# Order around the row maxima of a fused attention and expert kernel: two maxima and their places in the gating, the fourth score unit, and the norm's transposes

## The chip, the cores and the metric

One NeuronCore of a Trainium2 chip runs the whole kernel. The metric is the device time of one execution in microseconds (us). TensorE is called PE here, VectorE DVE, ScalarE ACT, GpSimd POOL, and SyncE, which issues most of the DMAs, SP. L1087 is line 1087 of the kernel before.

## The reference, cut to what matters

The input is x of 32 batch elements x 256 positions x 128 channels, float32. A layer norm gives xn; the output is x + attention(xn) + ffn(xn).

```
def attention(xn):                       # 16 heads of width 8
    q, k, v = split(xn @ Wqkv.T)
    q, k = rotate(q, cos, sin), rotate(k, cos, sin)
    s = q @ k.T / sqrt(8) + decay_bias   # causal
    return softmax(s) @ v @ Wo.T

def ffn(x):
    n1 = layernorm(x)
    rw = gating(n1, smha_sim)            # 8 experts, thresholded cosine, top 2 as fallback, softmax
    q, k, v = (einsum(n1, w, rw) for w in (q_proj, k_proj, v_proj))
    hs = x + einsum(softmax(causal(q @ k.T / sqrt(128))) @ v, o_proj, rw)
    n2 = layernorm(hs)
    rw2 = gating(n2, moe_sim)
    return hs + einsum(gelu(n2 @ w1), w2, rw2)
```

## The kernel before

The kernel is written for each engine as a program of its own, with semaphores between them; the order on each engine is the order of the code. The batch elements pass through a pipeline. `step(n, u, n_x)` is written once for each engine; n is the element, u its parity, and n_x says which later elements still exist (3: all; 29 of the 32 steps). Two steps stand in a hardware loop.

In step n the softmax attention and the expert attention of element n are finished, the row maxima of element n+1 are taken, the gating of element n+2 is worked out, and the norm and the rotated q and k of element n+3 are made.

The 16-head attention takes its scores twice. `unit1` on PE puts scores in PSUM banks S1, and `row_max` on DVE (L1087) reads them; six units of both, numbered 0 to 5, make up an element. A unit needs the S1 banks empty, so PE's unit k+1 waits for DVE's maximum k (`s1_read`), and the maximum k+1 waits for PE (`s1_out`). `max_parts` splits the maxima, and they are fed back as rows of the operands. `unit2` on PE then puts the scores less maxima in banks S2, ACT takes `exp_slot` (L674) and puts the masks back with `seed_slot` (L680); `unit2` k waits for the seed k-1. After three of these `pv` (L1437, L1442) multiplies by v: half 0 and half 1. `ve`, `qk` and `oe` are the weight products of the expert attention, `soft_max` (L1122 to L1125), `soft_exp` (L699, L701) and `soft_T` its softmax.

On DVE the `gating` is a chain of 31 small dependent instructions ("links"; 128x16 elements). `beside_gating(k)` is called behind link k and puts other work between: one instruction of the layer norm's own chain (`layer_norm`, a generator), a row maximum where k stands in `GATE_MAX_AT`, the soft maximum at 15, the normalising of PV's first half at 18. The layer norm's last link, L917, releases POOL's `second_norm` (L572, a product of two SBUF tiles, and the copy L576). `rotate` (L1004 to L1014) turns q and k of element n+3 and splits them into three bf16 parts that SP stores. PE's `norm_T` (L1329) transposes the new norm into bank S1[0], ACT's `evac_norm_x` (L620) copies it to xzT, and `proj` (L1337) and `proj_v` (L1360) multiply it by the weights. At the end of a step DVE's `add_x` waits for `att_out`, and then come `rotate`, the row maximum 0 of the next step's element, and `add_hs` (L1154, L1161).

Of the kernel before, what the change touches and what calls it, by code (L numbers as in the profile page):

```python
# [24 lines left out]
UNITS = 3 * NQ  # L25
# [33 lines left out]
MAX_LINKS = 3  # L59
ATS_CHUNKS = ((0, 1), (1, 1), (2, 2), (4, 2), (6, 2))  # L60
GELU_AT = (2, 7, 12, 17, 22, 27)
GATE_MAX_AT = (2, 7, 11, 14, 17)


class Chain:
# [55 lines left out]
def build(nc, x, w_attn, w_o, log_xi, pi_logit, e_logit, ln1_w, ln1_b, ln2_w, ln2_b, sim1, gates1,  # L121
# [9 lines left out]
    with ExitStack() as ctx:  # L131
# [468 lines left out]
        def _(act):  # L600
# [16 lines left out]

            def evac_norm_x(b, banks):
                act.wait_ge(xzT_out, b + 1)
                act.activation(xzT[:], ps[:, banks[0]].rearrange("p (a t) -> p a t", a=2), ACT.Copy).then_inc(xnT_done, 1)  # L620

            def evac_norm_1(b, par):
# [60 lines left out]
            def exps(n, k):  # L683
                exp_slot(n, k)
                seed_slot(n, k)

            def evac_pv(n, Q):
                act.wait_ge(pv_out, NQ * n + Q + 1)
                act.wait_ge(ot_out, NQ * n + max(Q - 1, 0))
                act.activation(ov[:, Q], ps[:, PVB, 0:S], ACT.Copy).then_inc(ov_done, 1)  # L690

            def evac_qk(n):
                act.wait_ge(qk_out, n + 1)
                act.activation(qT[:], ps[:, QKB, 0:S], ACT.Copy, scale=D ** -0.5).then_inc(qkT_done, 1)
                act.activation(kT[:], ps[:, QKB, S:2 * S], ACT.Copy).then_inc(qkT_done, 1)
# [74 lines left out]
            def step(n, u, n_x):  # L770
                if n_x >= 2:
                    evac_norm_1(n + 2, u)
                exps(n, 0)
                if n_x >= 2:
                    evac_logits(n + 2)
                if n_x == 0:
                    evac_norm2(0)
                    square2(0)
                exps(n, 1)
                if n_x == 0:  # L780
                    evac_norm2(1)
                    square2(1)
                exps(n, 2)
                if n_x == 0:
                    scale_norm2(2)
                    evac_logits2(0)
                evac_qk(n)
                evac_pv(n, 0)
                exps(n, 3)
                if n_x == 0:  # L790
                    scale_norm2(3)
                if n_x >= 2:
                    gate_tanh(n + 2)
                soft_exp(n)
                exps(n, 4)
                if n_x == 0:
                    evac_norm2(2)
                    square2(2)
                    gate_tanh2(0)
                exp_slot(n, 5)  # L800
                evac_soft(n)
                evac_ve(n)
                if n_x:
                    seed_slot(n, 5)
                if n_x == 0:
                    evac_norm2(3)
                    square2(3)
                evac_pv(n, 1)
                if n_x == 3:
                    evac_norm_x(n + 3, LATER)  # L810
                if n_x >= 2:
                    evac_v(n + 2, u)
                if n_x >= 2:
                    evac_weights(n + 2)
                if n_x:
                    evac_max(n + 1)
                evac_att(n)
                if n_x:
                    put_max(n + 1, 1 - u)
                if n_x == 1:  # L820
                    scale_norm2(0)
                    scale_norm2(1)
                if n_x == 0:
                    evac_weights2(0)
                    evac_logits2(1)
# [60 lines left out]
        def _(dve):  # L886
# [113 lines left out]
            def rotate(b, banks):  # L1000
                c = Chain(dve, rot_chain, b, ROT_LINKS)
                both = ps[:, banks[1]].rearrange("p (a t) -> p a t", a=2)
                dve.wait_ge(rot_out, b + 1)
                c.add(dve.tensor_tensor(rott, both, cs[:, :, 0], ALU.mult))  # L1004
                c.add(dve.stream_shuffle(swapped, both, SWAP))
                c.wait()
                c.link(dve.tensor_tensor(swapped, swapped, cs[:, :, 1], ALU.mult))
                c.link(dve.tensor_tensor(rot, rott, swapped, ALU.add))

                dve.wait_ge(parts_stored, 32 * b)  # L1010
                c.link(dve.tensor_copy(parts[:, 0], rot))
                c.link(dve.tensor_tensor(rres, rot, parts[:, 0], ALU.subtract))
                c.link(dve.tensor_copy(parts[:, 1], rres))
                dve.tensor_tensor(parts[:, 2], rres, parts[:, 1], ALU.subtract).then_inc(parts_out, 1)  # L1014
                c.close()
# [62 lines left out]
            def row_max(b, k):  # L1078

                Q, i = divmod(k, 3)  # L1080
                dve.wait_ge(s1_out, UNITS * b + k + 1)
                if k == 0:

                    dve.wait_ge(max_chain, (MAX_LINKS + 1) * b)
                n = HG if i == 0 else 2
                h = HG * Q + (0 if i < 2 else 2)
                dve.tensor_reduce(mx[:, min(i, 1)].rearrange("p (f h) -> p f h", f=NF)[:, :, h:h + n],  # L1087
                                  ps[:, S1[0]:S1[0] + NF].rearrange("p f (h t) -> p f h t", h=n),
                                  AX_X, ALU.max, negate=True).then_inc(s1_read, 1)
# [105 lines left out]
            def step(n, u, n_x):  # L1195
                def next_max(k):
                    if n_x:
                        row_max(n + 1, k)


                norm = (layer_norm(n + 3, 1 - u) if n_x == 3 else layer_norm2(0) if n_x == 1 else
                        layer_norm2(1) if n_x == 0 else iter(()))

                def beside_gating(k):
                    next(norm, None)
                    if k in GATE_MAX_AT:
                        next_max(1 + GATE_MAX_AT.index(k))
                    if k == 15:
                        soft_max(n)
                    if k == 18:  # L1210
                        normalise(n, 0)
                    if k == 28:
                        soft_norm(n)
                if n_x >= 2:
                    for _ in range(3):
                        next(norm, None)
                    gating(n + 2, T, 0, gate1, LG1, NORM1, 1, beside_gating)
                    run(norm)
                else:
                    if n_x == 0:  # L1220
                        run(norm)
                        gating(0, BP, 1, gate2, LG2(0), LG2(0)[:, :, E], 2, beside_gating)
                        run(layer_norm2(2))
                    else:
                        for k in range(1, GATE_LINKS + 1):
                            beside_gating(k)
                        run(norm)
                if n_x:
                    max_parts(n + 1)
                normalise(n, 1)  # L1230
                for e, ne in ATS_CHUNKS:
                    scale_att(n, u, e, ne)
                add_x(n, u)
                if n_x == 3:
                    rotate(n + 3, LATER)
                if n_x >= 2:
                    row_max(n + 2, 0)
                add_hs(n, u)

            for b in range(2):  # L1240
                norm = layer_norm(b + 1, 1 - b)
                rotate(b, FIRST)
                gating(b, T, 0, gate1, LG1, NORM1, 1, lambda k, norm=norm: next(norm, None))
                run(norm)
            for k in range(UNITS):
                row_max(0, k)
            max_parts(0)
            rotate(2, LATER)
            row_max(1, 0)
            step(0, 0, 3)  # L1250
            step(1, 1, 3)
            with dve.Fori(1, NB // 2 - 2) as j:
# [59 lines left out]
        def _(pe):  # L1312
# [173 lines left out]
            def soft_T(n):  # L1486
                pe.wait_ge(sexp_done, 2 * n + 2)
                for k in range(3):
                    ins = pe.transpose(ps[:, G1, k * P:(k + 1) * P], sp[:, k * P:(k + 1) * P], ident[:])
                ins.then_inc(spT_out, 1)  # L1490
# [79 lines left out]
            def step(n, u, n_x):  # L1570
# [28 lines left out]
                qk(n, 6)  # L1599
                next_max(3)  # L1600
                qk(n, 7)
                pv(n, u, 0)
                if n_x == 0:
                    logits2(0)
                next_max(4)
                unit2(n, u, 3)
                soft_scores(n)
                ve(n, 0)
                out_T(n, 0)
# [10 lines left out]
                if n_x == 0:  # L1620
                    norm_T2(3)
                soft_T(n)
                pv(n, u, 1)
                soft_av(n, (lambda: pe.wait_ge(lg_read, f + 1)) if n_x >= 2 else (lambda: None))
                out_T(n, 1)
                if n_x >= 2:
                    proj_v(f, True)
                if n_x == 3:

                    norm_T(g, LATER, lambda: pe.wait_ge(s1_read, UNITS * f))  # L1630
                if n_x >= 2:

                    weights_T(f, lambda: None)
# [147 lines left out]
```

## Time and profile before

| | us |
|---|---|
| median of 3 runs (1326.6 to 1327.27) | 1326.93 |
| the profiled execution | 1325.18 |
| its span, first to last instruction | 1323.4 |
| PE busy (10652 matmuls) | 1172.0, 89% |
| DVE busy | 1029.2, 78% |
| ACT busy | 713.0, 54% |
| POOL busy | 211.5, 16% |

The mean granted clock of TensorE is 0.975 of full speed. The span has three parts: about 90 us of setting up and first elements, the 32 steps to about 1035 us, and then the expert MLP. Busy shares are over the whole span; what sets the time of the steps must be read from one of them.

### The profile page before, as it was taken

The numbers are of one execution on the slowest core, as the hardware profiler recorded it, in microseconds if no ns is written. First come the engines' busy times: TensorE is split into PE (matmuls) and PEld (weight loads), VectorE is DVE, ScalarE is ACT, GpSimd is POOL, SyncE is SP. The second block draws the span as 40 slices with busy tenths as digits, with TensorE's granted clock in tenths as the row PEclk, the third lists the DMA queues.
The fourth block names the chain that finished last, engine by engine and source line by source line (L and its number), as shares of the span: only waits on it lengthen the run. The fifth ranks groups of instructions, "written<-read, shape, count | busy, mean of one in ns | idle before, by whom it ended". The sixth has DMA issues, their size and how long they took to land.

```text
span 1323.4 us, 33513 instructions
## 1 busy us (share of the span) xinstructions
PE 1172.0 (89%) x10652; PEld 900.1 (68%) x10652; DVE 1029.2 (78%) x3723; ACT 713.0 (54%) x1281; POOL 211.5 (16%) x325
## 2 busy tenths in 40 slices
PE   0239999999999999999999999999999979999998
PEld 0117777777777777777777777777777757777776
DVE  6568888888888888888888888888887567777664
ACT  1106655566665556565556665555665855555532
POOL 1021111211122211111221112221111100000000
PEclk9659999999999999999999999999999999999999
DMA  5221333323333332233333233333223034444453
GB/s 136 76 82 43 86 101 103 91 84 86 84 83 86 85 87 81 81 91 99 103 83 87 85 83 84 86 86 85 81 82 114 11 148 161 161 160 161 162 194 141
DMA packets 107941, 133.18 MB, mean 101 GB/s; under 512 B 18116, under 2 KB 87252, under 8 KB 99692
## 3 DMA queue, kind: packets, MB, share of 16 engines
q1 hardware_dynamic: 105668, 131.66, 33.1%
q10 hardware_dynamic: 2216, 0.80, 0.2%
q8 instruction: 31, 0.51, 0.2%
q14 instruction: 26, 0.21, 0.1%
HBM read 109.12 MB, written 21.54 MB: 99 GB/s over the span
## 4 chain that ended last, share of the span: by engine, by line
PE 58%; DVE 18%; ACT 9%; issue 7%; SPq 4%; DMA 2%; DVEq 1%; ACTq 0%
PE ps L1712 9%; PE ps L1698 8%; ACT pr L674 5%; PE ps L1437 5%; PE ps L1460 5%; PE ps L1461 4%; DVE mx L1087 3%; PE ps L1470 3%; PE ps L1506 3%; PE ps L1337 3%; ACT ps L680 3%; PE ps L1442 2%; PE ps L1386 2%; SPq L417 2%; PE ps L1396 2%
## 5 line engine op out<-in xcount | busy, mean ns | idle before, releaser
L674 ACT ACTIVATE pr<-ps 128x1024 f32<-128x1024 f32 x192 | 196.5, 1023 | 159.1 <-PE ps L1420 87.7
L1087 DVE TENSOR_REDUCE mx<-ps 128x4 f32<-128x1024 f32 (+1 forms) x192 | 234.8, 1223 | 56.3 <-PE ps L1396 48.3
L565 POOL TENSOR_TENSOR n1s<-rep,n1T 128x256 f32<-128x256 f32 x256 | 177.4, 729 | 365.7 <-DVE mpart L1101 345.8
L680 ACT ACTIVATE ps<-trn 128x1024 f32<-128x1024 bf16 x191 | 196.6, 1029 | 5.1
L1712 PEld LDWEIGHTS ps<-w2s,ats 128*128 128x128 f32 x1024 | 131.7, 192 | 51.3 <-issue 46.5
L1460 PE MATMUL ps<-n1s,wqk 128*128 128x256 f32 x512 | 163.6, 401 | 0.0
L1461 PE MATMUL ps<-n1s,wqk 128*128 128x256 f32 x512 | 152.9, 380 | 0.0
L858 ACT ACTIVATE n1s<-ps 128x512 f32<-128x512 f32 x128 | 76.5, 597 | 123.2 <-PE ps L1698 122.0
L1470 PE MATMUL ps<-wv,n1s 128*128 128x128 f32 x1024 | 141.6, 281 | 0.0
L1712 PE MATMUL ps<-w2s,ats 128*128 128x128 f32 x1024 | 135.8, 276 | 1.7 <-DVE ats L1269 1.7
L1470 PEld LDWEIGHTS ps<-wv,n1s 128*128 128x128 f32 x1024 | 126.7, 191 | 11.5 <-issue 6.5
L1698 PE MATMUL ps<-rep,w1s 128*128 128x512 f32 x256 | 130.7, 594 | 0.0
L1506 PE MATMUL ps<-wop,ats 128*128 128x128 f32 x1024 | 127.5, 278 | 0.2 <-DVE ats L1138 0.2
L1506 PEld LDWEIGHTS ps<-wop,ats 128*128 128x128 f32 x1024 | 120.9, 193 | 5.6 <-issue 4.9
L1461 PEld LDWEIGHTS ps<-n1s,wqk 128*128 128x128 f32 x512 | 97.8, 191 | 13.5
L1460 PEld LDWEIGHTS ps<-n1s,wqk 128*128 128x128 f32 x512 | 89.0, 194 | 20.8 <-issue 7.6
L572 POOL TENSOR_TENSOR zt<-xn,rstd 128x256 f32<-128x256 f32 x32 | 19.6, 612 | 461.0 <-DVE rstd L917 461.0
L1138 DVE TENSOR_TENSOR ats<-rep,ps 128x512 f32<-128x512 f32 (+1 forms) x160 | 81.1, 573 | 0.0
L1386 PE MATMUL ps<-mask_r,mask_l 64*128 64x256 bf16 x256 | 36.6, 283 | 46.9 <-DVE mx L1087 46.6
L1437 PE MATMUL ps<-pr,vst 128*32 128x256 f32 x1024 | 68.5, 385 | 7.3 <-ACT pr L674 6.6
L1386 PEld LDWEIGHTS ps<-mask_r,mask_l 64*128 64x128 bf16 x256 | 12.3, 93 | 78.7 <-DVE mx L1087 68.0
L620 ACT ACTIVATE xzT<-ps 128x512 f32<-128x512 f32 x32 | 19.1, 597 | 78.4 <-PE ps L1329 78.4
(229 smaller groups left out, 2031.9 us busy)
## 6 DMA issues: line engine op xcount, KB each, us to landing
rep<-scr_rw SPq DMA_DIRECT2D x32, 1024.0 KB, 5.7
stk<-scr_rw SPq DMA_DIRECT2D x16, 1024.0 KB, 8.3
stk<-scr_parts SPq DMA_DIRECT2D x896, 16.0 KB
scr_parts<-parts SPq DMA_DIRECT2D x64, 192.0 KB, 5.9
rots<-scr_rw SPq DMA_DIRECT2D x8, 1024.0 KB, 4.8
wqk<-scr_rw SPq DMA_DIRECT2D x8, 1024.0 KB, 9.1
stk<-scr_parts SPq DMA_DIRECT2D x128, 48.0 KB
xt<-in_x SPq DMA_DIRECT2D x32, 128.0 KB, 2.1
```

The costliest lines, as they stand in the source:

```text
L565: pool.tensor_tensor(n1s[:, e], rep[:, par, e], n1T[:, par], ALU.mult).then_inc(n1s_done, 1)
L674: act.activation(pr[:, Q, :, i], ps[:, S2[0]:S2[0] + NF], ACT.Exp).then_inc(exp_done, 1)
L680: act.activation(ps[:, S2[0]:S2[0] + NF], seeds[:, kind:kind + 1].broadcast_to((P, NF, 512)), ACT.Copy).then_inc(seed_done, 1)
L1087: dve.tensor_reduce(mx[:, min(i, 1)].rearrange("p (f h) -> p f h", f=NF)[:, :, h:h + n], ps[:, S1[0]:S1[0] + NF].rearrange("p f (h t) -> p ...
L1138: dve.tensor_tensor(ats[:, e:e + ne], rep[:, u, e:e + ne], ps[:, G0:G0 + 1, 0:S].broadcast_to((P, ne, S)), ALU.mult).then_inc(ats_done, 1)
L1437: mm(ps[32 * h:32 * h + 32, PVB, 0:S], vst[:, u, 0, HH * f + HG * Q + h], pr[:, Q, f, h // 2, (h % 2) * S:(h % 2 + 1) * S], start=(f == 0) ...
L1460: mm(ps[:, QKB, 0:S], wq[:, e], n1s[:, e], start=(e == 0), stop=(e == E - 1), skip_group_check=True)
L1461: ins = mm(ps[:, QKB, S:2 * S], wk[:, e], n1s[:, e], start=False, stop=(e == E - 1), skip_group_check=True)
L1470: ins = mm(ps[:, QKB, i * D:(i + 1) * D], n1s[:, e, i * P:(i + 1) * P], wv[:, e], start=(e == 0 and i == 0), stop=(e == E - 1), skip_group ...
L1506: ins = mm(ps[:, G1, i * D:(i + 1) * D], ats[:, e, i * P:(i + 1) * P], wop[:, e], start=(e == 0 and i == 0), stop=(e == E - 1), skip_group ...
L1698: mm(ps[:, UP[k % 4]], w1s[:, e], n2T[t % 8], start=True, stop=True).then_inc(up_out, 1)
L1712: ins = mm(ps[:, MOE[t % 2], i * D:(i + 1) * D], hgs[:, k % 2, i * P:(i + 1) * P], w2s[:, e], start=(e == 0 and i == 0), stop=(e == E - 1) ...
```

## The change

The instructions stay the same. What moves:

- DVE: row maximum 0 goes between the rotation and the bf16 parts. `rotate` becomes a generator with one `yield` for this.
- DVE: row maximum 1 goes ahead of the layer norm's statistics and the gating. The maxima 2 to 5 stand behind links 1, 6, 13 and 17; before, 1 to 5 stood behind 2, 7, 11, 14 and 17.
- PE: `unit2` 3 goes ahead of `pv` 0, and `norm_T` ahead of `pv` 1.
- ACT: exponential 3 goes ahead of the copy of `pv` 0, its seed stays behind it. `evac_norm_x` also waits for `proj_v` (`v_out`), which reads the old xzT.

```diff
-GATE_MAX_AT = (2, 7, 11, 14, 17)
+GATE_MAX_AT = (1, 6, 13, 17)
...
             def evac_norm_x(b, banks):
                 act.wait_ge(xzT_out, b + 1)
+
+                act.wait_ge(v_out, b)
...
                 evac_qk(n)
+                exp_slot(n, 3)
                 evac_pv(n, 0)
-                exps(n, 3)
+                seed_slot(n, 3)
...
                 c.link(dve.tensor_tensor(rot, rott, swapped, ALU.add))
+                yield
 
                 dve.wait_ge(parts_stored, 32 * b)
                 c.link(dve.tensor_copy(parts[:, 0], rot))
...
+                next_max(1)
                 norm = (layer_norm(n + 3, 1 - u) if n_x == 3 else layer_norm2(0) if n_x == 1 else
                         layer_norm2(1) if n_x == 0 else iter(()))
 
                 def beside_gating(k):
                     next(norm, None)
                     if k in GATE_MAX_AT:
-                        next_max(1 + GATE_MAX_AT.index(k))
+                        next_max(2 + GATE_MAX_AT.index(k))
...
                 add_x(n, u)
-                if n_x == 3:
-                    rotate(n + 3, LATER)
+                turn = rotate(n + 3, LATER) if n_x == 3 else iter(())
+                next(turn, None)
                 if n_x >= 2:
                     row_max(n + 2, 0)
+                run(turn)
                 add_hs(n, u)
...
                 qk(n, 7)
+                unit2(n, u, 3)
                 pv(n, u, 0)
                 if n_x == 0:
                     logits2(0)
                 next_max(4)
-                unit2(n, u, 3)
                 soft_scores(n)
...
                 soft_T(n)
+                if n_x == 3:
+
+                    norm_T(g, LATER, lambda: pe.wait_ge(s1_read, UNITS * f))
                 pv(n, u, 1)
                 soft_av(n, (lambda: pe.wait_ge(lg_read, f + 1)) if n_x >= 2 else (lambda: None))
                 out_T(n, 1)
                 if n_x >= 2:
                     proj_v(f, True)
-                if n_x == 3:
-
-                    norm_T(g, LATER, lambda: pe.wait_ge(s1_read, UNITS * f))
```

The setting up has the same turn of `rotate` and `row_max` for its first elements. The changed file is up to eight lines longer ahead of a given place, so its line numbers are 2 to 8 higher.

On DVE, from the end of the rotation over the residual to the next step's first statistics, before: `rots` and `parts` are the rotated values and their bf16 parts, `mx` the row maxima, `hs` and `bs` the residual, `bst` the statistics.

```order
288 L1008 TENSOR_TENSOR rots<-rots 128x512
289 L1011 CAST parts<-rots 128x512
290 L1012 TENSOR_TENSOR rots<-rots,parts 128x512
291 L1013 CAST parts<-rots 128x512
292 L1014 TENSOR_TENSOR parts<-rots,parts 128x512
293 L1087 TENSOR_REDUCE mx<-ps 128x2x4
294 L1154 SCALAR_TENSOR_TENSOR hs<-ps,smx,hs 128x128 x2
295 L1161 TENSOR_TENSOR bs<-hs,xa 128x256
296 L897 BN_STATS bst<-xt 128x6 x2
```

And of the change:

```order
288 L1011 TENSOR_TENSOR rots<-rots 128x512
289 L1091 TENSOR_REDUCE mx<-ps 128x2x4
290 L1015 CAST parts<-rots 128x512
291 L1016 TENSOR_TENSOR rots<-rots,parts 128x512
292 L1017 CAST parts<-rots 128x512
293 L1018 TENSOR_TENSOR parts<-rots,parts 128x512
294 L1158 SCALAR_TENSOR_TENSOR hs<-ps,smx,hs 128x128 x2
295 L1165 TENSOR_TENSOR bs<-hs,xa 128x256
296 L1091 TENSOR_REDUCE mx<-ps 128x2x2
297 L900 BN_STATS bst<-xt 128x6 x2
```

Maximum 0 has moved ahead of the four instructions of the parts, and maximum 1 stands directly behind the residual.

On DVE, around the end of the layer norm's chain inside the gating, before: `rstd` is the norm's last result, `gs` and `gt` the gating's small tiles, `smx` the soft maximum.

```order
241 L917 TENSOR_TENSOR rstd<-vstd,rstd 128x2
242 L1087 TENSOR_REDUCE mx<-ps 128x2x4
243 L1034 TENSOR_TENSOR gt<-ps,gs 128x16
244 L1036 TENSOR_TENSOR gt<-gt,sg 128x16
245 L1037 TENSOR_REDUCE gs<-gt 128x2
246 L1038 TENSOR_TENSOR gt<-gt,gs 128x16
247 L1040 SCALAR_TENSOR_TENSOR gt<-gt,rank 128x16
248 L1087 TENSOR_REDUCE mx<-ps 128x2x2
249 L1041 TENSOR_REDUCE gs<-gt 128x2
250 L1122 TENSOR_REDUCE smx<-ps 128x1
```

And of the change:

```order
242 L920 TENSOR_TENSOR rstd<-vstd,rstd 128x2
243 L1038 TENSOR_TENSOR gt<-ps,gs 128x16
244 L1040 TENSOR_TENSOR gt<-gt,sg 128x16
245 L1041 TENSOR_REDUCE gs<-gt 128x2
246 L1091 TENSOR_REDUCE mx<-ps 128x2x2
247 L1042 TENSOR_TENSOR gt<-gt,gs 128x16
248 L1044 SCALAR_TENSOR_TENSOR gt<-gt,rank 128x16
249 L1045 TENSOR_REDUCE gs<-gt 128x2
250 L1126 TENSOR_REDUCE smx<-ps 128x1
```

No maximum stands behind the norm's last link any more, and maximum 4 stands ahead of two more links than before (1038 and 1040 of before, 1042 and 1044 now).

On PE, at the end of the `ve` products, before: `sp` is the soft softmax, `pr` the exponentials, `xn` and `zt` the new norm.

```order
82 L1489 MATMUL ps<-ident,sp 128x128 x3
83 L1437 MATMUL ps<-pr,vst 32x256 x8
84 L1442 MATMUL ps<-pr,vst 32x128 x8
85 L1496 MATMUL ps<-spT,vs 128x256
86 L1497 MATMUL ps<-spT,vs 128x128
87 L1449 MATMUL ps<-ident,ov 128x128 x2
88 L1360 MATMUL ps<-wa,xzT 128x128 x2
89 L1329 MATMUL ps<-ident,xn 128x128 x2
90 L1329 MATMUL ps<-ident,zt 128x128 x2
```

And of the change:

```order
82 L1497 MATMUL ps<-ident,sp 128x128 x3
83 L1337 MATMUL ps<-ident,xn 128x128 x2
84 L1337 MATMUL ps<-ident,zt 128x128 x2
85 L1445 MATMUL ps<-pr,vst 32x256 x8
86 L1450 MATMUL ps<-pr,vst 32x128 x8
```

The norm's four transposes have moved from behind `proj_v` to the front of the second PV half.

## Rows read from the trace of the kernel before

**Rows 1.** Busy time by stretches: from:to, length, then us (and instructions) by engine

```profile
160.00:465.00 305.00, 283.43 (x2806) 222.54 (x2804) 257.97 (x938) 181.20 (x320) 64.81 (x100) 1.00 0.32 88
```

**Rows 2.** Timeline of ACT, the copy to xzT: start, length, [idle before <-releaser]

```profile
490.23 0.60 ACT L620 ACTIVATE xzT<-ps 128x512 f32<-128x512 f32 x1 [1.54 <-PE ps L1329]
...
551.56 0.60 ACT L620 ACTIVATE xzT<-ps 128x512 f32<-128x512 f32 x1 [1.54 <-PE ps L1329]
```

**Rows 3.** Waits of PE, 160 to 770 us: total, times, longest

```profile
PE ps L1386 <- DVE mx L1087: 30.0, 40, 1.4
```

**Rows 4.** Timeline of DVE, end of a step

```profile
526.40 0.69 DVE L1008 TENSOR_TENSOR rots<-rots 128x512 f32<-128x512 f32 x1
...
529.48 1.22 DVE L1087 TENSOR_REDUCE mx<-ps 128x8 f32<-128x1024 f32 x1
```

**Rows 5.** Timeline of DVE, layer norm, gating, soft maximum

```profile
501.14 0.48 DVE L897 BATCH_NORM_STATS2 bst<-xt 128x6 f32<-128x128 f32 x2
...
502.79 1.23 DVE L1087 TENSOR_REDUCE mx<-ps 128x4 f32<-128x1024 f32 x1
...
507.34 0.16 DVE L917 TENSOR_TENSOR rstd<-vstd,rstd 128x2 f32<-128x2 f32 x1
507.45 1.23 DVE L1087 TENSOR_REDUCE mx<-ps 128x8 f32<-128x1024 f32 x1
...
510.24 1.22 DVE L1087 TENSOR_REDUCE mx<-ps 128x4 f32<-128x1024 f32 x1 [0.65 <-PE ps L1396]
...
511.46 0.28 DVE L1122 TENSOR_REDUCE smx<-ps 128x1 f32<-128x128 f32 x1
...
512.10 0.17 DVE L1125 TENSOR_SCALAR smx<-smx 128x2 f32<-128x2 f32 x1
```

**Rows 6.** Timeline of PE in the same step; PEld is the weight load

```profile
504.07 0.28 PE L1386 MATMUL ps<-mask_r,mask_l 64*128 64x256 bf16 x2 [1.15 <-DVE mx L1087]
...
509.81 0.38 PE L1396 MATMUL ps<-stk 64*128 64x256 bf16 x4
...
510.34 0.10 PEld L1480 LDWEIGHTS ps<-mask_qk,identb 128*128 128x128 bf16 x1 [0.21 <-issue]
...
515.68 0.40 PE L1423 MATMUL ps<-stk 64*128 64x128 bf16 x8 [0.20 <-ACT ps L680]
...
516.55 0.49 PE L1489 MATMUL ps<-ident,sp 128*128 128x128 f32 x3
517.27 1.07 PE L1437 MATMUL ps<-pr,vst 128*32 128x256 f32 x16 [0.23 <-ACT pr L674]
...
519.68 0.61 PE L1360 MATMUL ps<-wa,xzT 128*128 128x128 f32 x4
520.13 0.38 PE L1329 MATMUL ps<-ident,xn 128*128 128x128 f32 x2
...
521.42 0.48 PE L1337 MATMUL ps<-xzT,wa 128*128 128x256 f32 x1 [0.24 <-ACT xzT L620]
```

**Rows 7.** Timeline of ACT: fourth seed, soft exponentials

```profile
511.51 1.03 ACT L680 ACTIVATE ps<-trn 128x1024 f32<-128x1024 bf16 x1
...
512.58 0.35 ACT L699 ACTIVATE sp<-ps,smx 128x128 f32<-128x128 f32 x1
```

**Rows 8.** Timeline of POOL, the second norm in the same step

```profile
507.58 0.61 POOL L572 TENSOR_TENSOR zt<-xn,rstd 128x256 f32<-128x256 f32 x1 [13.61 <-DVE rstd L917]
```

**Rows 9.** Line 1042: durations, ns, least, median, most

```profile
L1042 DVE TENSOR_TENSOR gt<-gt,gs x40: 167/176/486, 44.7 to 1272.2; 128x16 f32<-128x16 f32 x32, 128x64 f32<-128x64 f32 x8
```

**Rows 10.** Timelines of DVE and POOL in the prologue

```profile
71.87 0.49 DVE L1042 TENSOR_TENSOR gt<-gt,gs 128x16 f32<-128x16 f32 x1
72.39 0.30 DVE L1043 SCALAR_TENSOR_TENSOR gt<-gt 128x16 f32<-128x16 f32 x1
...
71.72 0.61 POOL L572 TENSOR_TENSOR zt<-xn,rstd 128x256 f32<-128x256 f32 x1 [26.25 <-DVE rstd L917]
72.27 0.40 POOL L576 COPY hs<-xn 128x256 f32<-128x256 f32 x1
```

More of the change, by code:

```diff
@@ L1241, in _ @@
                 norm = layer_norm(b + 1, 1 - b)
-                rotate(b, FIRST)
+                run(rotate(b, FIRST))
                 gating(b, T, 0, gate1, LG1, NORM1, 1, lambda k, norm=norm: next(norm, None))
@@ L1247, in _ @@
             max_parts(0)
-            rotate(2, LATER)
+            turn = rotate(2, LATER)
+            next(turn)
             row_max(1, 0)
+            run(turn)
             step(0, 0, 3)
```

## The prediction

> **What bounds the kernel now.** I read the table by stretches first, to see how full each engine is. In the steady part, 160 to 465 us, the granted clock is 1.00 and TensorE (PE) is busy 283.43 of 305 us [rows 1], so the most that any reordering can give there is 7%. The vector engine (DVE) is busy 257.97. The part behind 1035 us, the expert MLP, has none of the changed code. Then the period: the activation of line 620 starts once per batch element, at 490.23 and, two elements later, at 551.56 [rows 2]. That is 61.33 for two, 30.54 and 30.79 by turns; where the pair begins anew, the loop's edge costs DVE 0.25.
>
> Then the waits. Over 20 elements, 160 to 770 us, PE waits 30.0 us for the row maxima of L1087, 1.5 each [rows 3]. But these maxima in their turn wait for PE's scores, as the timeline of one element shows: neither engine alone sets the period, they hand it to each other. I use the timeline's own times; for the end of the element before, take 30.54 off.
>
> DVE adds x, turns the new q and k (L1008 at 526.40), splits them into bf16 parts and only then takes row maximum 0 at 529.48 [rows 4]. It goes on with the residual, the layer norm's statistics (L897 at 501.14) and the first links of the gating, and takes maximum 1 at 502.79 [rows 5]. PE has stood for 1.15 us before its scores of unit 2 at 504.07 [rows 6]. This is the stall that the new order touches first. From there PE runs on to the scores of unit 4, for which DVE waits 0.65 before 510.24 [rows 5]. ACT works off exponential 3, its seed, the soft exponentials at 512.58 and exponential 4 [rows 7]; PE takes the fourth seed at 515.68, and at 517.27 starts the second PV half [rows 6].
>
> **The change part by part.** No instruction is added or removed; only order and one wait change.
>
> *DVE, the two maxima.* Row maximum 0 goes right behind L1008, which ends at 527.1: 2.3 us earlier than 529.48 [rows 4]; the parts then end about where the maximum ended before. Maximum 1 takes L897's place behind the residual, at about 501.2 instead of 502.79 [rows 5], ending at 502.4 instead of 504.02. PE reaches unit 2 at 504.07 - 1.15 = 502.9 [rows 6], or 0.2 earlier if the wait before unit 1 is a true one. So PE's stall goes, and PE runs 1.15 to 1.36 ahead. Taken alone this is 1.2 x 30 = 36 us.
>
> *Where it goes.* DVE does all of its other work between L1008 and the soft maximum as before. That path is 511.46 - (526.40 - 30.54) = 15.60 us, of which the wait of 0.65 is the only gap of note [rows 4, 5]. The maxima take their 1.22 wherever they stand. So however early PE is, DVE's path can shrink by 0.65 at most. The split parts go to DMAs which SP issues only when the next element's residual is there; that and the DMAs' own order don't change.
>
> *A new neighbour.* Row maximum 3 now covers the two GpSimd (POOL) instructions of the second norm: L917 starts at 507.34, POOL's product of two SBUF tiles at 507.58 for 0.61, and the maximum at 507.45, which reads PSUM, runs over both [rows 5, 8]. With the new table of places maximum 3 comes five gating links earlier. Behind L917 stand L1034, then L1036, which reads two SBUF tiles. L1034 can start 0.11 behind L917, as maximum 3 does now [rows 5], and a link starts 0.03 behind the end of the one before (L1043 behind L1042 [rows 10]), so L1036 another 0.20 on: 0.31 behind L917. POOL's product starts 0.24 behind L917, first by 0.07. The trace has such a meeting in the prologue: L1042, also gt and gs from SBUF, starts at 71.87 under POOL's product of 71.72 to 72.33 and takes 0.49, and L1043 under POOL's copy takes 0.30 [rows 10]; the median of L1042 is 0.176 [rows 9]. L1042 ended as POOL's product did. For L1036 this gives 0.24 + 0.61 - 0.31 = 0.54 to the product's end and 0.03 behind it, 0.40 more than the 0.17 of such a link. Bounds: nothing, if it starts ahead of POOL; and 0.72, if it sits through the copy as well. I take 0.40, since the prologue's row is the same meeting.
>
> This is also what the Trainium skill says (SBUF — State Buffer, section "SBUF: two separate sides"): a DVE instruction with two SBUF inputs and a GpSimd instruction that reads SBUF take an exclusive lock for the whole instruction, and the loser blocks. The trace agrees, with 0.49 against 0.18. By the rule too, whichever starts first wins, which is the lower bound.
>
> DVE's sum up to the soft maximum: -0.65 + 0.40, and 0.12 for places where a maximum no longer covers the 0.2 us between two dependent links (an estimate from the spacing of the rows) = -0.13. L1038 and L1040 now stand behind maximum 4, but in place of the wait. The order needs PE's unit 4 by 509.7. PE's ended at 510.19 (L1396 [rows 6]); less 1.36, plus 0.32 for unit 3 ahead of PV and 0.2 for one more change of array tiling (0.21 of "issue" before L1480 is such a change [rows 6]), that is 509.35. So DVE does not wait there.
>
> *ACT.* Exponential 3 goes ahead of PV's copy and follows PE's lead of over 1 us, so its seed no longer stands in front of the soft exponentials: the seed of 511.51 ended at 512.54 and held L699 to 512.58, though the soft maximum was there at 512.27 [rows 5, 7]. Now L699 starts at 512.27 - 0.13 + 0.05 = 512.19, 0.39 earlier, and with it exponential 4, seed 4 and unit 5 (515.68 to 515.29). PE arrives there about 1.1 early: its stall has moved here.
>
> *Norm transposes.* The four of L1329 cost 0.44 (two are done 0.22 after 520.13 [rows 6], the others as much later). They go between soft_T and PV 1. Soft_T's end moves to 517.04 - 0.39 = 516.65; plus 0.44 and the 0.23 that PV's start takes = 517.32, against 517.27: no later. Behind it PE lacks the 0.44. The new wait on v_out lets L620 start when proj_v ends, at 519.68 + 0.61 = 520.3 [rows 6]; queued behind L620 on ACT are the v, weight, max and att copies, which all start 0.35 to 0.4 earlier than now. So L620, which takes 0.60 [rows 2], has xzT there at 521.0. The projection starts at 521.05 instead of 521.42 [rows 6]: **0.37 per element**. The max and att transposes lie between and are through by then. Att_out, and so DVE's add_x, which waits for it, follow, and the ring closes.
>
> 30 elements have the gating (29 with all stages, one without the new norm): 30 x 0.37 = 11.1 us. The profiled execution took 1325.18 us with a span of 1323.4; the median of the runs is 1326.93, 1.75 above it. The 11.1 is taken off both: 1314.1 for the profile, **1316** for the median.
>
> **Rivals.**
> 1. *L1036 starts ahead of POOL, or isn't held.* The margin is 0.07. DVE is then bound by PE's unit 4: maximum 4 some 0.27 earlier, soft exponentials 0.66 earlier, projection 0.62. 30 x 0.62 = 18.6: 1308. Against it: the prologue's row.
> 2. *L1036 sits through both POOL instructions*, 0.32 more: 0.05 per element, 1325. For it: POOL's copy starts 0.06 ahead of the product's end, at 72.27, and could be served first [rows 10]. Against it: L1042 was let in between.
> 3. *DVE does not set it, PE does*: all stalls of PE (1.5 for L1087 [rows 3], 0.20 for the seed, 0.23 for PV, 0.24 for xzT [rows 6]) less 0.2 for the tiling, at most 2.0, and 1.4 if the changes of tiling in these waits stay: 1267 to 1285. It needs a soft maximum 1 us earlier, and DVE has only 0.65 of gap; nothing speaks for it. A part of it, with gaps that I count as work, gives 1295 to 1303.
> 4. *Slower.* Maximum 4 now stands ahead of L1038, L1040, L1041 and the soft maximum, which before were partly done while DVE waited. If PE does not come early to unit 4, its scores end at 510.19 + 0.52 = 510.7; behind them come 1.22 as now (510.24 to 511.46), 0.41 for two links and 0.81 to the soft maximum's end [rows 5]: 513.2. The soft exponentials then start 0.68 later than now: 30 x 0.68 = 20, 1347. It decides as soon as PE's lead at unit 4 is under about 0.65 of my 1.36. For it: the seeds on ACT could hold PE. Against it: ACT's share of the stretch is 181.20 of 305 [rows 1], and its seeds follow PE's own earlier start.
> 5. *The change does nothing*, 1327: PE's stall only changes place. It needs DVE's path 0.4 longer than my sum.
>
> **How the numbers follow.** From no change one can tell here about 0.2%, 2.7 us. Chances: the forecast (1311 to 1321) 0.44; rival 1 (1303 to 1311) 0.22; rival 2 (1321 to 1326) 0.11; rival 3 and its part (under 1303) 0.07; rivals 4 and 5 0.16, of which 0.06 within 0.2%. Rival 2 lies half in "faster", half in "same". So faster 0.78, same 0.12, slower 0.10. The range of 8 in 10 leaves out rival 3 below, and the slower cases above: 1303 to 1326. The likeliest case alone has 1311 to 1321.
>
> **What would show it.** Right: PE's wait for L1087 falls from 1.5 to under 0.3 per element; DVE's wait of 0.65 before maximum 4 is gone; L1036 takes 0.5 to 0.6 instead of 0.17; PE waits about 1 us for the seed before L1423's group (unit 5), up from 0.2; L699 is released by DVE's L1125; the period is 30.2 and 30.4. Wrong: L1036 at 0.17 and a period under 30 (rival 1); maximum 4 waiting for PE by a microsecond (rival 4); or PE not waiting at all before unit 5 (rival 3).

## The result, and the profile after

The changed kernel takes 1295.36 us (median of 4 runs, 1294.61 to 1295.71) against 1326.76 (4 runs): ratio 0.976, 95% interval 0.975 to 0.978. That is 31.4 us faster. 1316 was forecast, with 1303 to 1326 for 8 in 10: the way is right, the size is a third of the true one, and the range doesn't hold the time.

The busy table of the changed kernel for the stretch of [rows 1]:

```profile
160.00:465.00 305.00, 296.70 (x2910) 230.36 (x2909) 269.65 (x971) 186.60 (x327) 65.03 (x100) 1.00 0.34 92
```

PE is busy 13 us more in the same 305, since more elements pass; the clock is 1.00 as before. The copy to xzT, for [rows 2]:

```profile
478.07 0.60 ACT L622 ACTIVATE xzT<-ps 128x512 f32<-128x512 f32 x1 [1.16 <-PE ps L1368]
...
536.99 0.60 ACT L622 ACTIVATE xzT<-ps 128x512 f32<-128x512 f32 x1 [1.16 <-PE ps L1368]
```

Two elements take 58.92 instead of 61.33, so 1.20 less for each; the forecast was 0.37. The waits of PE, DVE and ACT, 160 to 770 us, for [rows 3]:

```profile
PE ps L1431 <- ACT ps L682: 15.5, 21, 0.9
...
DVE mx L1091 <- PE ps L1401: 4.5, 21, 0.2
...
ACT sp L701 <- DVE smx L1129: 19.5, 21, 0.9
```

PE's 30.0 us of waiting for the row maxima are gone. In their place it waits 15.5 us for the fourth seed (L682), and ACT waits 0.93 for the soft maximum in each step. DVE waits before no maximum but the first. This is the ring of the prediction, DVE's soft maximum, ACT, PE's unit 5. The ring and the wait in it are as forecast; the sizes of the pieces are not. They are read from the same places of one step (starts, then lengths):

```profile
481.27 0.42 DVE L1149 TENSOR_TENSOR xa<-xr,ps 128x256 f32<-128x256 f32 x1 [0.61 <-PE ps L1528]
...
499.06 0.28 DVE L1126 TENSOR_REDUCE smx<-ps 128x1 f32<-128x128 f32 x1
...
510.90 0.42 DVE L1149 TENSOR_TENSOR xa<-xr,ps 128x256 f32<-128x256 f32 x1 [0.61 <-PE ps L1528]
```

```profile
499.91 0.37 ACT L701 ACTIVATE sp<-ps,smx 128x128 f32<-128x128 f32 x1 [0.93 <-DVE smx L1129]
...
500.71 1.02 ACT L676 ACTIVATE pr<-ps 128x1024 f32<-128x1024 f32 x1
...
503.29 1.02 ACT L676 ACTIVATE pr<-ps 128x1024 f32<-128x1024 f32 x1 [0.49 <-PE ps L1431]
```

```profile
502.85 0.40 PE L1431 MATMUL ps<-stk 64*128 64x128 bf16 x8 [0.94 <-ACT ps L682]
...
503.73 0.49 PE L1497 MATMUL ps<-ident,sp 128*128 128x128 f32 x3
504.05 0.38 PE L1337 MATMUL ps<-ident,xn 128*128 128x128 f32 x2
504.27 0.38 PE L1337 MATMUL ps<-ident,zt 128*128 128x128 f32 x2
504.58 1.07 PE L1445 MATMUL ps<-pr,vst 128*32 128x256 f32 x16
...
508.35 1.13 PE L1345 MATMUL ps<-xzT,wa 128*128 128x256 f32 x4
```

These starts cut the ring into pieces that follow each other without a gap. The table has the length of each piece in the kernel before (first column; the period is its sum) and in others, in us per step; where the two steps of the loop differ, both. Each number is a difference of two starts. For before, the pieces come from the starts of [rows 5 to 7], 523.96 for add_x, and two that are not shown there, exponential 4 at 513.54 and exponential 5 at 516.11.

| piece, start to start | before | after | a1 | a2 | b1 | b2 | e4 |
|---|---|---|---|---|---|---|---|
| add_x to soft maximum | 18.28, 18.03 | 17.45, 17.78 | 17.45, 17.78 | 18.61, 18.35 | 18.37, 18.13 | 17.50, 17.90 | 16.96, 16.93 |
| to soft exponential | 1.12 | 0.85 | 0.85 | 0.85 | 1.12 | 0.85 | 0.85 |
| to exponential 4 | 0.96 | 0.81 | 0.81 | 1.01 | 0.96 | 0.81 | 0.91 |
| to exponential 5 | 2.58 | 2.57 | 2.57 | 2.58 | 2.58 | 2.58 | 2.57 |
| to PV 1 | 1.16 | 1.29 | 1.16 | 1.29 | 1.16 | 1.16 | 1.29 |
| to projection | 4.15 | 3.77 | 4.15 | 3.77 | 4.15 | 4.15 | 3.77 |
| to add_x | 2.54 | 2.55 | 2.55 | 2.55 | 2.55 | 2.55 | 2.55 |
| period | 30.79, 30.54 | 29.29, 29.62 | 29.53, 29.86 | 30.67, 30.41 | 30.88, 30.65 | 29.59, 29.98 | 28.91, 28.88 |

Of the 1.21 gained on the mean, 0.54 lies in DVE's piece, 0.27 and 0.15 in ACT's two (up to the soft exponential and up to exponential 4), and 0.25 is the transposes'. a1 has ACT's 0.27 and 0.15 too, with ACT's old order: both follow from DVE's part of the change.

### The profile page after: what moved, and what is told of

Its sections match the earlier page's. It is cut to its first block, busy times and chain, and to the rows that moved or that the text cites. A ratio compares the mean times of both kernels' runs of the same rounds, so it can differ in the third digit from the quotient of the medians.

```text
span 1292.7 us, 33541 instructions
## 1 busy us (share of the span) xinstructions
PE 1176.6 (91%) x10652; PEld 898.3 (69%) x10652; DVE 1031.1 (80%) x3723; ACT 708.6 (55%) x1281; POOL 212.1 (16%) x325
## 4 chain that ended last, share of the span: by engine, by line
PE 43%; DVE 26%; issue 15%; ACT 7%; SPq 5%; DVEq 3%; DMA 2%; ACTq 0%
PE ps L1720 9%; PE ps L1706 8%; PE ps L1514 4%; DVE mx L1091 3%; PE ps L1445 3%; PE ps L1345 3%; ACT ps L682 3%; ACT pr L676 3%; PE ps L1468 2%; SPq L417 2%; PE ps L1469 2%; PE ps L1504 2%; PE ps L1478 1%; DVE rots L1016 1%; DVE rots L1008 1%
## 5 line engine op out<-in xcount | busy, mean ns | idle before, releaser
L682 ACT ACTIVATE ps<-trn 128x1024 f32<-128x1024 bf16 x191 | 196.4, 1028 | 4.1
L1277 DVE TENSOR_TENSOR ats<-n1s,stk 128x512 f32<-128x512 f32 x64 | 44.1, 688 | 14.2 <-PE ps L1720 13.9
L1113 DVE RECIPROCAL rden<-ps 128x16 f32<-128x16 f32 x64 | 16.2, 253 | 48.2 <-PE ps L1457 48.2
```

Source lines behind the costliest of these rows:

```text
L682: act.activation(ps[:, S2[0]:S2[0] + NF], seeds[:, kind:kind + 1].broadcast_to((P, NF, 512)), ACT.Copy).then_inc(seed_done, 1)
```

## The experiments

The first theory, formed on the profile after: the ring sets the period, with the pieces above, and DVE's part of the change gives nearly all. The rival: the moves on PE and ACT carry a third or more. The kernels below differ from one of the two by the edit shown; times are medians with the ratio to the kernel before, timed beside them on the same chip (1325.5 for the a and e kernels, 1326.3 for b and c).

**DVE's part alone (a1).** The changed kernel with these put back:

```diff
-                act.wait_ge(v_out, b)
-                exp_slot(n, 3)
                 evac_pv(n, 0)
-                seed_slot(n, 3)
+                exps(n, 3)
...
-                unit2(n, u, 3)
                 pv(n, u, 0)
                 next_max(4)
+                unit2(n, u, 3)
...
-                    norm_T(g, LATER, lambda: pe.wait_ge(s1_read, UNITS * f))    # ahead of pv 1
+                    norm_T(g, LATER, lambda: pe.wait_ge(s1_read, UNITS * f))    # behind proj_v
```

> DVE's part of the change alone: both row maxima early and the new places in the gating; the orders of PE and ACT as before. Theory (a ring DVE soft maximum, ACT, PE unit 5, PV 1, add_x, DVE sets the period, and the gain is DVE's path shorter by 0.6, the soft exponentials no longer behind the seed 0.27, exponential 4 no longer waiting for PE's unit 4, 0.16): about 1.0 us per step, 1297 us, and PE's wait for L1087 gone. Rival (PE's and ACT's moves carry a third of the gain or more, through the earlier unit 3 and exponential 3): 1306 us or more.

1300.32 us, ratio 0.981 (0.979 to 0.982): 25 of the 31 us. The rival is out. It is 3 us slower than the theory gave, though its period is 0.97 less, as expected. About 2 of the 3 us are lost ahead of the steady steps: the copy to xzT of 122.89 comes at 124.86 in a1. The rest is that only 28 intervals gain the 0.97.

**PE's and ACT's part alone (a2).** `row_max` 0 and 1 and `GATE_MAX_AT` as before, the rest as changed.

> PE's and ACT's part alone: unit 3 ahead of PV 0, exponential 3 ahead of PV's copy, the norm's transposes ahead of PV 1; DVE's order as before. Theory: unit 4's scores come 0.5 later to a DVE that waits for them, which costs 0.1 to 0.3 per step, the transposes give 0.24 back: 1321 to 1327 us. Rival (the moves carry a third or more): under 1316 us.

1323.26 us, ratio 0.998 (0.997 to 0.999), as the theory gave. PE's unit 4 behind unit 3 and PV makes DVE's soft maximum 0.33 later, and the transposes and ACT's order give that back and 0.13 more.

**Without the transposes' move (a3).** The changed kernel with `norm_T` behind `proj_v` and without the wait on `v_out`.

> The changed kernel with the norm's transposes put back behind proj_v and without ACT's new wait. Theory (the transposes fill PE's wait for exponential 5, costing 0.14 there and giving 0.38 later): 0.24 per step slower than the changed kernel, 1302 to 1303 us. Rival (they cost at PV 1 what they give back, as predicted before the result): 1295 to 1297 us.

1300.41 us, ratio 0.981 (0.979 to 0.983), 1.6 us under the bound of the theory and over the rival's 1297; the changed kernel has 0.976. So the move is worth about 6 us, 0.25 in each step, and the step of the prediction that let it cost 0.44 in front of PV 1 is refuted.

**Without unit 3 and exponential 3 (a4).** The changed kernel with `unit2` 3 behind `next_max(4)` and `exps(n, 3)` behind PV's copy.

> The changed kernel with unit 3 and exponential 3 put back. Theory (the soft exponentials wait 0.93 for DVE's soft maximum, so an earlier seed 3 changes nothing): 1294 to 1297 us. Rival (the earlier exponential 3 is what frees the soft exponentials): 1303 us or more, and the soft exponentials released by the seed, not by DVE.

1294.54 us, ratio 0.977 (0.975 to 0.978), the same as the changed kernel. In a4 ACT still waits for the soft maximum (14.8 us in 21 steps of the stretch), so the seed that exponential 3 frees is early for nobody. This part of the change gives nothing.

**Row maximum 0 alone (b1).** The kernel before, with only `rotate` split and `row_max` 0 between.

> Only row maximum 0 moved ahead of the bf16 parts; all else as before. Theory: maximum 1 stays where it was on DVE, so PE's stall before unit 2 only grows by what PE gains before unit 1; the ring is unchanged: 1324 to 1328 us. Rival (the early maximum 0 is half of the gain, as PE gets its banks 2.3 us earlier): 1316 us or less.

1328.92 us, ratio 1.002 (1.001 to 1.003), 0.9 us over the bound of the theory. The path to the soft maximum is 0.1 longer. The early maximum 0 gives nothing by itself; it costs some 2 us.

**Row maximum 1 and the new places of 2 to 5 (b2).** a1, but with maximum 0 behind the parts again.

> Only row maximum 1 moved ahead of the statistics, with the new places of 2 to 5; maximum 0 stays behind the parts, PE and ACT as before. Theory: PE's unit 1 is done before DVE has finished the residual, so this alone gives all that DVE's part gives: 1299 to 1302 us. Rival (maximum 1 would wait for PE's unit 1, which still waits for the late maximum 0): 1306 us or more, with a wait of DVE before the second maximum.

1303.17 us, ratio 0.982 (0.981 to 0.984), 1 us over the bound of the theory and far from the rival's. Maximum 1 and the new places together give 23 of DVE's 25 us; no run moves one without the other, so their shares stay open. Maximum 0 in front of the parts adds 0.05 and 0.12 in the two steps of the loop (a1 against b2 in the table). The 0.12 is a wait: in b2 DVE stands 0.16 for PE before maximum 3 in every second step, in a1 it does not.

**The held link (c1, c2).** In the changed kernel the two-input link behind the norm's chain, L1040, takes 0.57 in one step of the loop and 0.17 in the other. Timelines of DVE and POOL:

```profile
496.40 0.16 DVE L920 TENSOR_TENSOR rstd<-vstd,rstd 128x2 f32<-128x2 f32 x1
...
496.72 0.57 DVE L1040 TENSOR_TENSOR gt<-gt,sg 128x16 f32<-128x16 f32 x1
...
526.10 0.16 DVE L920 TENSOR_TENSOR rstd<-vstd,rstd 128x2 f32<-128x2 f32 x1
...
526.41 0.17 DVE L1040 TENSOR_TENSOR gt<-gt,sg 128x16 f32<-128x16 f32 x1
```

```profile
496.64 0.61 POOL L572 TENSOR_TENSOR zt<-xn,rstd 128x256 f32<-128x256 f32 x1 [14.95 <-DVE rstd L920]
...
526.42 0.65 POOL L572 TENSOR_TENSOR zt<-xn,rstd 128x256 f32<-128x256 f32 x1 [15.09 <-DVE rstd L920]
```

The link starts 0.32 and 0.31 behind L920. POOL's product starts 0.24 behind it in one step, first by 0.08, and the link ends 0.04 behind the product. In the other it starts 0.32 behind, 0.01 too late, and the link goes through; the product takes 0.65. If that is the cause, a link a little later loses in both. c1 delays it by a tiny instruction, c2 is the control with the same instruction elsewhere.

```diff
+        pad = sb("pad", [P, 2])
...
+                dve.memset(pad[:], 0.0)            # c1: ahead of L1038
                 dve.tensor_tensor(L, lg[:, :, 0:E], bc(gs[:, 6, 0:nt]), ALU.mult).then_inc(lg_read, 1)
...
+                dve.memset(pad[:], 0.0)            # c2: ahead of L1035
                 c.link(dve.tensor_scalar(rn, norm, NORM2, None, ALU.max))
```

> The changed kernel with one tiny DVE memset (128x2, of a tile that nothing reads) ahead of line 1038 of the changed kernel, that is between the norm's last link and the two-input link 1040, which then starts some 0.06 to 0.1 us later, behind the start of POOL's product. Theory (at present the link wins by 0.01 us; a later one is held to the product's end): line 1040 takes about 0.5 us and each step costs 0.1 + 0.35 to 0.4: 1306 to 1311 us. Rival (POOL never holds this link): line 1040 stays at 0.17 and the kernel is 2 to 4 us slower than the changed one, 1297 to 1299 us.

> Control for the price of the memset alone: the same memset ahead of the gating's first link, on the same path of DVE but before both the norm's last link and POOL's product, so that their distance stays. Both theories: 2 to 4 us slower than the changed kernel, 1297 to 1299 us, with line 1040 at 0.17 us.

c1: 1302.83 us, ratio 0.982 (0.980 to 0.984). c2: 1296.96, ratio 0.978 (0.976 to 0.979). The link's line, first in c1, then in c2 (durations in ns, least, median, most):

```profile
L1042 DVE TENSOR_TENSOR gt<-gt,sg x40: 174/536/632, 43.4 to 1248.5; 128x16 f32<-128x16 f32 x32, 128x64 f32<-128x64 f32 x8
```

```profile
L1042 DVE TENSOR_TENSOR gt<-gt,sg x40: 174/224/605, 43.5 to 1242.5; 128x16 f32<-128x16 f32 x32, 128x64 f32<-128x64 f32 x8
```

In c1 all 29 links that meet a product in the steps are held; in c2 and in the changed kernel it is 16 of 29, in the steady steps every second one. The same instruction costs 6 us more where it brings the link behind POOL's start. Where the link is held anew the path grows by 0.48 (17.45 to 17.93): the link starts 0.04 later against L920's counterpart, and its successor comes 0.44 later behind it. The closest meeting in c1 has the link 0.01 behind the product, and it is held as well:

```profile
172.92 0.63 DVE L1042 TENSOR_TENSOR gt<-gt,sg 128x16 f32<-128x16 f32 x1
...
172.91 0.62 POOL L573 TENSOR_TENSOR zt<-xn,rstd 128x256 f32<-128x256 f32 x1 [14.91 <-DVE rstd L921]
```

The hold is shown, and so is its price. I expected 1306 to 1311 for c1, since I took all steps as not held. In the step that is held already the path grows by 0.12 (17.78 to 17.90), but it does so in c2 too. In both kernels the 0.12 comes up at the norm's xn product, which starts 0.23 behind the link before it instead of 0.11. In c1 that is ahead of the added instruction, so it is neither the hold nor the instruction's own time; its cause is open.

**The ring's weakest place (e1 to e4).** If DVE's path to the soft maximum sets the period, bringing the soft maximum itself forward is worth its full shift. On DVE it stood behind three small instructions, L1042, L1044 and L1045 (L1042 is outside the count of links, the others are 14 and 15). Of these only L1042 releases another engine, ACT's small tanh:

```diff
-                    if k == 15:
+                    if k == 13:                    # e1, e2, e4
                         soft_max(n)
...
-                if n_x >= 2:
-                    gate_tanh(n + 2)
                 soft_exp(n)
+                if n_x >= 2:
+                    gate_tanh(n + 2)               # e2, e4
...
-GATE_MAX_AT = (1, 6, 13, 17)
+GATE_MAX_AT = (1, 6, 11, 17)                       # e3, e4; unit 3 and exponential 3 as in a4
```

> The changed kernel with the soft maximum right behind row maximum 4 (at link 13 instead of 15). Theory (DVE's path to the soft maximum sets the period, but ACT's small tanh stands ahead of the soft exponentials and waits for link 1042, which now comes behind the soft maximum): 0.1 to 0.2 per step faster, 1289 to 1293 us. Rival (the period is set elsewhere, by PE or the DMAs, once PE's stall is gone): within 2 us of the changed kernel, 1294 to 1297 us.

> As e1, and the tanh behind the soft exponentials on ACT. Theory: the soft exponentials follow the soft maximum at 0.85 us again, 0.41 earlier, less 0.1 for the tanh ahead of exponential 4: 1284 to 1288 us, and PE's wait for seed 4 falls from 0.78 by as much. Rival: as for e1, 1294 to 1297 us.

> The changed kernel with unit 3 and exponential 3 put back and row maximum 4 right behind the norm's last link (at 11), so that it covers POOL's two instructions, and no link with two SBUF inputs meets them. Theory (every second step pays 0.39 for the held link): DVE's path is even in all steps, 0.2 per step faster on the mean, 1287 to 1290 us, line 1040 at 0.17 in all steps. Rival (maximum 4 there waits for PE's unit 4 by more than the hold): 1295 us or more, with a wait of DVE before it.

> e2 and e3 together. Theory: their gains add up as long as PE still waits for seed 4 (0.78 now, 0.5 taken): 1278 to 1283 us. Rival (another bound comes first, PE's own work or the row maxima): 1286 us or more.

e1: 1285.18 us, ratio 0.970 (0.968 to 0.972). e2: 1282.23, ratio 0.968 (0.966 to 0.969). Both are better than I gave, and the path to the soft maximum is 0.5 shorter (16.95 and 17.29), not 0.41: I had counted two links, but the three instructions' starts took 0.20, 0.21 and 0.09 of the path. In e1 the soft exponentials start 1.07 behind it, held by the tanh; in e2 0.85.

e3: 1293.81 us, ratio 0.976 (0.974 to 0.978). This missed: maximum 4 covers POOL's product and no link is held, but the path is 17.58 and 17.55. The mean is 0.05 below the changed kernel's where 0.2 was expected. The timelines of e3, DVE's and POOL's:

```profile
526.95 1.23 DVE L1090 TENSOR_REDUCE mx<-ps 128x4 f32<-128x1024 f32 x1
528.09 0.17 DVE L1037 TENSOR_TENSOR gt<-ps,gs 128x16 f32<-128x16 f32 x1
528.29 0.18 DVE L1039 TENSOR_TENSOR gt<-gt,sg 128x16 f32<-128x16 f32 x1
528.50 0.17 DVE L1040 TENSOR_REDUCE gs<-gt 128x2 f32<-128x16 f32 x1
528.70 0.18 DVE L1041 TENSOR_TENSOR gt<-gt,gs 128x16 f32<-128x16 f32 x1
```

```profile
527.15 0.61 POOL L572 TENSOR_TENSOR zt<-xn,rstd 128x256 f32<-128x256 f32 x1 [15.17 <-DVE rstd L919]
```

Dependent links start 0.20 apart. In the changed kernel a maximum starts 0.09 behind the link L1041 and runs over the rest of its latency; in e3 it stands between the two chains, where 0.11 was the spacing anyway, and L1041's successor now waits its full 0.20. What the hold took, 0.39 in every second step, is mostly eaten by this: 0.13 in the step that was not held (17.45 to 17.58), some 0.16 in the other.

e4: 1278.21 us (1277.71 to 1279.34), ratio 0.965 (0.963 to 0.966). It beats the kernel before by 47 us and the changed one, by the two ratios, by about 15. PE's waits in e4 over the same stretch:

```profile
PE ps L1430 <- ACT ps L682: 6.2, 21, 0.3
```

PE's busy time is 301.13 of 305 there, and only 0.3 per step is left of its wait, so PE itself is nearly the bound.

## Why the prediction was wrong

The stall went where the prediction put it, from the maxima to the fourth seed. ACT waits for DVE's soft maximum, and the ring is DVE, ACT, PE. What failed are three terms of the sum: DVE's path (0.41 too little), the start of exponential 4 (0.15 too little) and the price of the transposes (0.27 too much). With the forecast's 0.37 they make 1.20 of the measured 1.21. A fourth point had the right size, but not the cause it was given.

- *"DVE's sum up to the soft maximum: -0.65 + 0.40, and 0.12 ... = -0.13".* It is -0.54 on the mean. First, the 0.40 is right in size (0.39) but is paid in one step of two: 0.20 of the gap. I read the margin of 0.07 from one step. POOL's product starts 0.24 behind L917 in one step of the loop and 0.32 in the other, in the trace of the kernel before as well; the second step would have shown a margin of -0.01 (rows below). Second, the 0.12 for uncovered links does not exist here, since maximum 4 still stands behind a single dependent link; e3, where it doesn't, pays 0.13 and more. Third, the loop's edge cost DVE 0.25 in every second step, and I carried it over: with maximum 1 behind it the edge is worth 0.07 (17.45, against 17.78 - 0.40 = 17.38 for a step that isn't held), 0.09 on the mean.
- *"L699 starts ... 0.39 earlier, and with it exponential 4".* The soft exponential gains what was said, 0.27, beside DVE's share. Exponential 4 gains 0.15 more. I took its 0.96 as ACT's own work. It started at 513.54, just behind the end of PE's unit 4 (rows below), and the chain of waits of the kernel before goes through that place from PE to ACT. In a2, where PE's unit 4 comes later, the piece grows to 1.01; where DVE's part lets PE come early (a1), it is 0.81.
- *"plus 0.44 and the 0.23 that PV's start takes = 517.32 ... no later".* Exponential 5 to PV 1 went from 1.16 to 1.29, while PV moved with exponential 5 by all that was gained ahead of it. The 0.23 before PV 1 was a wait for ACT, as its row says, and behind soft_T's end by starts (516.55 + 0.32 for three transposes) there were 0.40 to fill, not 0.23. The transposes took 0.13 of new time there and gave back 0.38 behind it, where I had 0.44 and 0.42. a3 shows the sum, 0.25 in each step.
- *"Exponential 3 goes ahead of PV's copy ..., so its seed no longer stands in front of the soft exponentials"*. The 0.27 came, but not from this: a1 and a4 have it with exponential 3 in its old place. PE's lead, which DVE's early maxima give, is enough by itself to have the seed done before the soft maximum.

The rows of the kernel before for the first two points, L917 and POOL's product in the other step of the loop, then PE's unit 4 and exponential 4:

```profile
538.13 0.16 DVE L917 TENSOR_TENSOR rstd<-vstd,rstd 128x2 f32<-128x2 f32 x1
...
538.45 0.61 POOL L572 TENSOR_TENSOR zt<-xn,rstd 128x256 f32<-128x256 f32 x1 [13.94 <-DVE rstd L917]
...
513.11 0.38 PE L1420 MATMUL ps<-stk 64*128 64x256 bf16 x4
...
513.54 1.02 ACT L674 ACTIVATE pr<-ps 128x1024 f32<-128x1024 f32 x1
```

Of the rivals, the first ("L1036 starts ahead of POOL, or isn't held") came true in half of the steps, and even its 1308 was short, because it shared the other terms. The part of rival 3, "with gaps that I count as work, gives 1295 to 1303", is what happened. It had a chance of 0.07 and was left out of the range, and PE does not set the period yet: it still waits for the seed. Rival 4 did not come: PE was early at unit 4.

The count of steps was a little high too. The first and the last copy to xzT inside the steps are 824.48 us apart (125.02 to 949.50), and were 857.51 (122.89 to 980.40): 28 intervals give 33.0 us, 1.18 each. The way to the first of these copies became 2.1 us longer, most of it in the first step, and from the last to the end it takes 0.2 more; this makes the 30.7 by which the spans differ. I did not look for the cause of the 2.1.

## What to carry to other kernels

When a stall is taken out of a ring of waits, cut the ring into pieces by the starts of one instruction on each engine, and ask of every piece which end of it is work and which is a wait on something that moves as well; here 0.15 (exponential 4) and 0.31 (0.44 less 0.13, in front of PV 1) hid in pieces that looked like work. In a loop that is written out twice, read both copies before a margin of some hundredths decides a term. And bring forward what the other engines wait for ahead of all that only its own engine needs: the soft maximum three small instructions earlier took the ratio from 0.976 to 0.970, some 8.5 us, more than a quarter of what the whole change gave.

## What was unexpected of the hardware

Whether a 0.17 us DVE instruction with two SBUF inputs takes 0.57 is decided by 0.01 or 0.02 us. At 526.41 it started ahead of POOL's product (526.42) and kept its 0.17, while the product took 0.65 instead of 0.61. At 172.92 in c1 it started 0.01 behind the product and took 0.63; at 496.72 it came 0.08 behind and ended 0.04 after the product's end.

The Trainium skill has the rule (SBUF — State Buffer, section "SBUF: two separate sides"): whichever of the two starts first gets the shared ports for the whole instruction, and the other is blocked. The trace agrees on who wins, and on the loser's wait where POOL wins. Where DVE wins, the product grows by 0.04 only, less than the link's 0.17, so the time for which a small DVE instruction holds the ports is not the time that its row shows.
